# Selection matrices compared with a row of numbers in PSUM, in a two-layer graph network kernel

## The chip, the cores and the metric

The kernel runs on one core of a Trainium2 chip. The metric is the device time of one execution in microseconds (us), start to end on that core; lower is better. The core has a matrix engine (TensorE, PE in the profile, its weight loads PEld), a vector engine (VectorE, DVE), a scalar engine (ScalarE, ACT), a general engine (GpSimd, POOL) which here mainly issues gathers from memory, and a queue that issues other transfers (SyncE, SP). SBUF is the on-chip memory, PSUM the smaller memory that TensorE writes its results to, in eight banks.

## What is computed

There are 12500 nodes with 64 features each and 212500 edges, sorted by destination. A first layer adds, for each node, the features of the sources of its edges and the edges' own features, and runs a small network and a batch norm on the sum. A second and a third layer are graph convolutions on the same edges. Cut to what matters:

```python
edge_index = jnp.stack([src, dst])
h = jnp.maximum(_layernorm(x), 0.0)
# layer 0
msg = h[src] + edge_attr_64
agg = jax.ops.segment_sum(msg, dst, num_segments=n)
y = jax.nn.relu(agg @ W1 + b1) @ W2 + b2
x = x + batch_norm(y)
h = jnp.maximum(_layernorm(x), 0.0)
# layer 1, twice: h -> relu(segment_sum((h @ W)[src] * enorm, dst) + b)
...
x = x + layer_norm_over_the_graph(h)
```

The edges' sum by destination is the work: it is done three times, once in each of three passes.

## The kernel before

Each of the three passes (numbered 0, 1 and 2) adds, for every node, the rows of its sources in two ways.

**Dense tiles.** For the first 54 tiles of 125 destination nodes in pass 0 (69 in passes 1 and 2) a matrix of counts, sources by destinations, is built and multiplied with the node rows held in SBUF. A tile has 25 slots. In a slot of a built tile DVE makes a pair of one-hot matrices (`oh`: L906 from `modT`, L907 from `keyT`), PE multiplies them (`bld`, L1030), and ACT copies the result to SBUF as a slice of the counts (`evict`, L1150). PE applies a finished tile's counts to the node rows, four matmuls in each slot (`app`, L1048). When a tile is done, DVE folds its three parts (`fold_v`, L947 and L948), PE turns the fold over (`turn`, L1135) into `ps_g`, the first 128 columns of PSUM bank 6, and DVE adds that to the sums in `acc` (`add`, L968).

**Groups.** The edges of the other nodes, and in pass 0 the edge features of all edges, go in groups of 1280 edges (128 partitions by 10). DVE makes a selection matrix `S` for a group (L917): 128 x 10 x 96 numbers, 1 where an edge's destination relative to the group's first is equal to the column's number. In pass 0 it also splits the edges' features in three parts (`rest1` and `rest2`, both L931). PE multiplies `S` with the edge features (L1063, pass 0) and with the gathered rows (L1070), ten matmuls each. POOL issues the gathers, ten to a group, into four buffers (L1212). DVE folds the result (`fold_q`, L938), PE turns it into `ps_g` (L1131), and DVE adds it to a window of `acc` (`add`, L964). Pass 0 has 167 groups, of which 79 gather; passes 1 and 2 have 54 each, and all gather.

**What sets the order.** `make_plan` gives each step of a pass a number in slots, and each engine's list is sorted by it. Each engine then works strictly down its list, with semaphore waits. For a group that PE takes at `t`, `S` stands at `t - 5.6`, `rest1` at `t - 5.2`, `rest2` at `t - 4.2`, `fold_q` at `t + 2.4`, its turn at `t + 4.6`, its add 2.1 behind the turn. A pair of one-hots stands 3.3 ahead of its build. A tile's fold stands 2.7 ahead of its turn or more. In pass 0 there are 1387 slots, and groups follow each other every 8.23 slots.

**Buffers that tie the engines.** There are four pairs of one-hots (`NOH`): DVE makes a pair once the build four before is done. There are three banks for builds (`NBANK`), two buffers of `S` (`NS`), two folds of each kind, and one `ps_g`, so a turn waits for the add before it.

## Time and profile before

| | |
|---|---|
| median of 3 runs | 4285.88 us |
| lowest, highest run | 4264.55, 4296.05 us |
| the profiled execution | 4260.3 us |
| its span, first to last instruction | 4258.7 us |
| PE, DVE, ACT, POOL busy in the span | 73%, 43%, 32%, 51% |
| granted TensorE clock, mean | 0.83 of full speed |

The profile is of one execution. Pass 0 lies between 160 and 1740 us of its span, pass 1 between 1880 and 3125, pass 2 between 3125 and 4215. A busy share over the whole span mixes these passes, in which different engines are loaded, so the windows by stage are to be read first. "Idle before" is the time in which an engine had nothing to run ahead of an instruction, and the name behind the arrow is what ended it; "issue" is time for which no releaser is seen, "remote" stands for one that the profile does not know.

### The profile page before, as it was taken

The numbers are of one execution on the slowest core, as the hardware profiler recorded it, in microseconds if no ns is written. First come the engines' busy times: TensorE is split into PE (matmuls) and PEld (weight loads), VectorE is DVE, ScalarE is ACT, GpSimd is POOL, SyncE is SP. The second block draws the span as 40 slices with busy tenths as digits, with TensorE's granted clock in tenths as the row PEclk, the third lists the DMA queues.
The fourth block names the chain that finished last, engine by engine and source line by source line (L and its number), as shares of the span: only waits on it lengthen the run. The fifth ranks groups of instructions, "written<-read, shape, count | busy, mean of one in ns | idle before, by whom it ended". The sixth has DMA issues, their size and how long they took to land.

```text
span 4258.7 us, 67106 instructions
## 1 busy us (share of the span) xinstructions
PE 3105.3 (73%) x25880; PEld 2681.6 (63%) x25880; DVE 1824.2 (43%) x5570; ACT 1353.1 (32%) x2188; POOL 2185.3 (51%) x1905
## 2 busy tenths in 40 slices
PE   2466877878777788557777787877847777777776
PEld 1245666666566676446776676766847766677666
DVE  7656777778676778612323232332201111111112
ACT  1345665656555666432223232222200000000001
POOL 5676777787767670034444444444144444444541
PEclk6678999989888899678878888888968878888888
DMA  3433444444444343543233333333543333333434
GB/s 65 103 104 103 127 123 127 121 113 130 115 106 123 108 131 110 110 136 127 92 134 102 122 127 101 132 103 118 163 123 116 123 126 118 122 128 117 135 116 128
DMA packets 396698, 503.75 MB, mean 118 GB/s; under 512 B 340668, under 2 KB 340732, under 8 KB 371676
## 3 DMA queue, kind: packets, MB, share of 16 engines
q1 hardware_dynamic: 323345, 402.81, 29.5%
q0 software_dynamic: 60416, 93.34, 9.0%
q10 hardware_dynamic: 12616, 3.20, 0.5%
q8 instruction: 216, 3.54, 0.3%
q14 instruction: 105, 0.86, 0.1%
HBM read 362.07 MB, written 137.13 MB: 117 GB/s over the span
## 4 chain that ended last, share of the span: by engine, by line
PE 53%; DVE 15%; another core or an unknown queue 12%; issue 12%; POOL 3%; ACT 2%; DVEq 1%; DMA 0%; SPq 0%; ACTq 0%; POOLq 0%
PE psum L1048 33%; PE psum L1030 8%; PE psum L1070 4%; DVE arena L907 4%; PE psum L1063 4%; DVE arena L917 3%; DVE arena L931 3%; DVE arena L906 2%; PE psum L1015 1%; POOL arena L1212 1%; ACT arena L1150 1%; DVEq L962 1%; PE psum L1135 1%; PE psum L1083 1%
## 5 line engine op out<-in xcount | busy, mean ns | idle before, releaser
L1212 POOL DMA_INDIRECT arena<-table,srcT x1840 | 2090.4, 1136 | 1709.7 <-PE psum L1070 1056.0
L1048 PE MATMUL psum<-arena 125*125 125x193 bf16 (+1 forms) x19200 | 2323.0, 266 | 369.0 <-issue 316.4
L1048 PEld LDWEIGHTS psum<-arena 125*125 125x125 fp8e4 x19200 | 2090.6, 151 | 609.7 <-issue 458.5
L1150 ACT ACTIVATE arena<-psum 125x500 fp8e4<-125x500 f32 x1775 | 1156.9, 709 | 1355.8 <-PE psum L1030 948.6
L1030 PE MATMUL psum<-arena 128*125 128x500 f16 x1775 | 735.9, 416 | 271.5 <-issue 108.1
L906 DVE TENSOR_SCALAR arena<-iota,modT 128x125 f16<-128x125 f16 x1775 | 468.3, 264 | 544.2 <-PE psum L1030 287.4
L907 DVE TENSOR_SCALAR arena<-iota,keyT 128x500 f16<-128x500 f16 x1775 | 617.3, 348 | 0.0
L1030 PEld LDWEIGHTS psum<-arena 128*125 128x125 f16 x1775 | 259.0, 146 | 377.7 <-DVE arena L907 193.4
L1194 ACT ACTIVATE cneg<-cst 125x1 f32<-125x1 f32 x25 | 5.1, 203 | 1135.4 <-DVE arena L987 950.8
L917 DVE TENSOR_TENSOR arena<-relT,iota 128x960 bf16<-128x960 f16 x272 | 311.2, 1144 | 0.0
L948 DVE TENSOR_REDUCE arena<-psum 125x64 f32<-125x192 f32 x192 | 67.1, 350 | 515.6 <-remote 302.8
L931 DVE TENSOR_TENSOR arena<-arena 128x650 f32<-128x650 f32 (+1 forms) x334 | 274.0, 820 | 0.9 <-DMA arena<-in_edge_attr_dram 0.8
L938 DVE TENSOR_REDUCE arena<-psum 96x65 f32<-96x195 f32 (+1 forms) x275 | 96.2, 350 | 272.0 <-PE psum L1070 268.6
L1070 PE MATMUL psum<-arena 128*96 128x192 bf16 x1846 | 198.8, 259 | 10.1 <-DMA arena<-table,srcT 9.9
L1063 PE MATMUL psum<-arena 128*96 128x195 bf16 (+1 forms) x1662 | 204.1, 275 | 2.1 <-DVE arena L931 1.7
L1135 PE MATMUL psum<-ident,arena 125*64 125x125 f32 x192 | 60.5, 315 | 197.0 <-DVE arena L948 97.1
L1063 PEld LDWEIGHTS psum<-arena 128*96 128x96 bf16 (+1 forms) x1662 | 181.2, 137 | 8.0 <-issue 5.8
L1070 PEld LDWEIGHTS psum<-arena 128*96 128x96 bf16 x1846 | 176.6, 132 | 11.8 <-DMA arena<-table,srcT 10.7
L968 DVE SCALAR_TENSOR_TENSOR acc<-psum,acc 64x125 f32<-64x125 f32 x192 | 53.3, 277 | 264.7 <-remote 171.9
L947 DVE COPY cnt<-psum 125x1 f32<-125x1 f32 x123 | 18.8, 153 | 341.5 <-remote 243.1
L1135 PEld LDWEIGHTS psum<-ident,arena 125*64 125x64 f32 x192 | 23.6, 123 | 219.1 <-issue 179.7
L964 DVE TENSOR_TENSOR acc<-acc,psum 65x96 f32 (+1 forms) x275 | 67.6, 246 | 191.6 <-PE psum L1131 141.4
(199 smaller groups left out, 1008.3 us busy)
## 6 DMA issues: line engine op xcount, KB each, us to landing
arena<-counts SPq DMA_DIRECT2D x121, 1600.0 KB
counts<-arena SPq DMA_DIRECT2D x71, 1600.0 KB
arena<-in_edge_attr_dram SPq DMA_DIRECT2D x166, 320.0 KB
arena<-table,srcT POOLq DMA_INDIRECT x1840
table<-arena SPq DMA_DIRECT2D x8, 1050.0 KB
table<-arena SPq DMA_DIRECT2D x25, 168.0 KB
arena<-table SPq DMA_DIRECT2D x4, 1050.0 KB
arena<-in_x_dram ACTq DMA_DIRECT2D x4, 700.0 KB
```

Source lines behind the costliest of these rows:

```text
L906: dve.tensor_scalar(ob(v % NOH), iota0[:, 0:PN], modT[:, v:v + 1], None, ALU.is_equal)
L907: dve.tensor_scalar(oh(v % NOH), iota1[:, :], keyT[:, v:v + 1], None, ALU.is_equal).then_inc(v_oh, 1)
L917: dve.tensor_tensor(S, rel, it, ALU.is_equal).then_inc(v_S, 1)
L931: dve.tensor_tensor(ebuf(e, i + 1)[0:parts, 0:nt * FE], a, upper, ALU.subtract).then_inc(v_rest1 if i == 0 else v_rest2, 1)
L938: dve.tensor_reduce(qbuf(n % 2)[:, 0:fe], ps_q.rearrange("p (s f) -> p f s", s=3)[:, 0:fe, :], X, ALU.add).then_inc(v_fq, 1)
L1030: pe.matmul(ps_b[v % NBANK][0:PN, :], ob(v % NOH), oh(v % NOH), start=True, stop=True).then_inc(p_bld, 1)
L1048: last = pe.matmul(ps_v[n % 2][0:PN, 0:xc], A(slot)[0:PN, j, 0:PN], Xs[0:PN, j, 0:xc], start=(j == 0), stop=(j == J - 1))
L1063: last = pe.matmul(ps_q, S[0:parts, t, :], e3(v % NEDGE)[0:parts, t, :, :], start=(t == 0), stop=(t == nt - 1 and not gathered))
L1070: last = pe.matmul(to, S[0:parts, t, :], gbuf(slot)[0:parts, t, :].rearrange("p (s f) -> p s f", s=3), start=(k > 0 and t == 0), stop=(t = ...
L1135: pe.transpose(ps_g[0:F, 0:PN], vbuf(m % 2)[0:PN, :], ident[0:PN, 0:PN]).then_inc(p_win, 1)
L1150: act.activation(A(slot)[0:PN, :, i * SUB:(i + 1) * SUB], ps_b[b % NBANK][0:PN, :].rearrange("p (j r) -> p j r", r=SUB), ACT.Copy, scale=S ...
L1212: pool.indirect_dma_start(out=gbuf(slot)[0:parts, t, :], out_offset=None, in_=tables[k], in_offset=bass.IndirectOffsetOnAxis(ap=idx, axis= ...
```

## The change

Four edits. First, a row of numbers 0 to 95 in 32-bit floats (`ps_i`) is written once into columns 256 to 351 of PSUM bank 6, beside `ps_g`. Second, `S` is made by a `scalar_tensor_tensor` that adds 0 to the relative destinations (16-bit, SBUF) and compares the result with `ps_i`, in place of a `tensor_tensor` on two 16-bit operands in SBUF. Third, since DVE now reads bank 6 for `S` and PE writes the turns there, `S` waits until PE has done the turn of the last fold that stands ahead of it in DVE's list, and `S` stands at `t - 7.0` in place of `t - 5.6`. Fourth, the add of a group takes the form that the add of a tile has: `scalar_tensor_tensor` with the PSUM operand first.

```diff
@@ make_plan
-        dve.append((t - 5.6, "S", n))
+        dve.append((t - 7.0, "S", n))
@@
         ps_g = psum[:, 6, 0:P]
+        ps_i = psum[:, 6, 2 * P:2 * P + W]
@@ dve_enter
+                V(dve.tensor_copy(ps_i, iota[:, 0:W]))
@@ dve_pass
-            for kind, v in half(pl, "dve", early):
+            whole = pl["dve"]
+            folded = [0]
+            for kind, v in whole:
+                u = pl["turn"]["grp" if kind == "fold_q" else "win", v] + 1 if kind in ("fold_q", "fold_v") else 0
+                folded.append(max(folded[-1], u))
+            first = 0 if early is not False else pl["early"]["dve"]
+            for at, (kind, v) in enumerate(half(pl, "dve", early), first):
@@ kind == "S"
                     if n >= NS:
                         dve.wait_ge(p_q, n - NS + 1)
+                    if folded[at]:
+                        dve.wait_ge(p_win, pl["u0"] + folded[at])
                     S = sbuf(n % NS)
                     if g < G:
                         rel = relT[:, :, g:g + 1].broadcast_to([P, NT, W])
-                        it = iota0[:, 0:W].rearrange("p (a w) -> p a w", a=1).broadcast_to([P, NT, W])
-                        dve.tensor_tensor(S, rel, it, ALU.is_equal).then_inc(v_S, 1)
+                        it = ps_i.rearrange("p (a w) -> p a w", a=1).broadcast_to([P, NT, W])
+                        dve.scalar_tensor_tensor(out=S, in0=rel, scalar=0.0, in1=it, op0=ALU.add,
+                                                 op1=ALU.is_equal).then_inc(v_S, 1)
...
@@ kind == "add"
-                        dve.tensor_tensor(win, win, ps_g[0:fe, 0:W], ALU.add).then_inc(v_add, 1)
+                        dve.scalar_tensor_tensor(out=win, in0=ps_g[0:fe, 0:W], scalar=1.0, in1=win, op0=ALU.mult,
+                                                 op1=ALU.add).then_inc(v_add, 1)
```

DVE's list in pass 0 around the `S` of group 75 (the groups counted from 0 in the order in which they are taken). Before:

```order
L906 TENSOR_SCALAR arena<-iota,modT 128x125
L907 TENSOR_SCALAR arena<-iota,keyT 128x500
L906 TENSOR_SCALAR arena<-iota,modT 128x125
L907 TENSOR_SCALAR arena<-iota,keyT 128x500
L938 TENSOR_REDUCE arena<-psum 96x65
L906 TENSOR_SCALAR arena<-iota,modT 128x125
L907 TENSOR_SCALAR arena<-iota,keyT 128x500
L917 TENSOR_TENSOR arena<-relT,iota 128x960
L931 TENSOR_TENSOR arena<-arena 128x650
L906 TENSOR_SCALAR arena<-iota,modT 128x125
L907 TENSOR_SCALAR arena<-iota,keyT 128x500
L931 TENSOR_TENSOR arena<-arena 128x650
```

And of the change, whose line numbers are higher by 8 to 13 (L914 and L915 are the pair, L927 is `S`, L950 `fold_q`, L943 the rests):

```order
L914 TENSOR_SCALAR arena<-iota,modT 128x125
L915 TENSOR_SCALAR arena<-iota,keyT 128x500
L927 SCALAR_TENSOR_TENSOR arena<-relT,psum 128x960
L914 TENSOR_SCALAR arena<-iota,modT 128x125
L915 TENSOR_SCALAR arena<-iota,keyT 128x500
L950 TENSOR_REDUCE arena<-psum 96x65
L914 TENSOR_SCALAR arena<-iota,modT 128x125
L915 TENSOR_SCALAR arena<-iota,keyT 128x500
L943 TENSOR_TENSOR arena<-arena 128x650
L914 TENSOR_SCALAR arena<-iota,modT 128x125
L915 TENSOR_SCALAR arena<-iota,keyT 128x500
L943 TENSOR_TENSOR arena<-arena 128x650
```

`S` has moved ahead of a pair of one-hots, of `fold_q` and of a second pair. Over pass 0 it moves ahead of two pairs for 65 of the 167 groups, of one pair for 99, and of none for 3.

DVE's list in pass 0 around the `S` of group 28, where a tile's fold stands near. Before (L947 and L948 are the tile's count and fold):

```order
L947 COPY cnt<-psum 125x1
L948 TENSOR_REDUCE arena<-psum 125x64
L906 TENSOR_SCALAR arena<-iota,modT 128x125
L907 TENSOR_SCALAR arena<-iota,keyT 128x500
L938 TENSOR_REDUCE arena<-psum 96x65
L906 TENSOR_SCALAR arena<-iota,modT 128x125
L907 TENSOR_SCALAR arena<-iota,keyT 128x500
L917 TENSOR_TENSOR arena<-relT,iota 128x960
```

And of the change (L959 and L960 are the tile's count and fold):

```order
L959 COPY cnt<-psum 125x1
L960 TENSOR_REDUCE arena<-psum 125x64
L927 SCALAR_TENSOR_TENSOR arena<-relT,psum 128x960
L914 TENSOR_SCALAR arena<-iota,modT 128x125
L915 TENSOR_SCALAR arena<-iota,keyT 128x500
L950 TENSOR_REDUCE arena<-psum 96x65
L914 TENSOR_SCALAR arena<-iota,modT 128x125
L915 TENSOR_SCALAR arena<-iota,keyT 128x500
```

`S` now stands right behind the tile's fold, so it waits there until PE has done that fold's turn. In 30 of the 167 groups of pass 0, and in 9 of the 54 of each later pass, `S` stands between a fold and the add behind its turn; in the others the wait is for a turn whose add DVE has already done.

## Rows read from the trace of the kernel before

**Rows 1.** Windows by stage: stretch, its length, busy us of each engine (instructions), granted clock.

```profile
160.00:1740.00 1580.00, 1229.76 (x9515) 985.37 (x9515) 1147.44 (x3703) 913.65 (x1493) 1065.97 (x783) 0.89 0.43 118
1880.00:3125.00 1245.00, 969.14 (x8389) 866.41 (x8389) 357.59 (x1301) 330.79 (x509) 491.50 (x507) 0.84 0.37 122
3125.00:4215.00 1090.00, 808.09 (x7410) 754.54 (x7411) 139.04 (x336) 17.68 (x66) 500.57 (x518) 0.82 0.37 122
```

**Rows 2.** Waits of PE in the first pass: us in total, times, longest us.

```profile
PE psum L1030 <- issue: 88.3, 68, 6.9
PE psum L1030 <- ACT arena L1150: 80.7, 57, 14.5
PE psum L1030 <- DVE arena L907: 62.4, 130, 4.5
...
PE psum L1070 <- DMA arena<-table,srcT: 9.9, 3, 5.8
```

**Rows 3.** Waits of DVE in the first pass, same columns.

```profile
DVE arena L906 <- PE psum L1030: 239.9, 202, 4.6
```

**Rows 4.** Waits of PE in the second and third pass, same columns.

```profile
PE psum L1048 <- issue: 295.3, 453, 2.5
...
PE psum L1030 <- DVE arena L907: 14.5, 9, 3.2
```

**Rows 5.** Page, costliest groups: count, busy us, mean ns, idle before and its releaser.

```profile
L1212 POOL DMA_INDIRECT arena<-table,srcT x1840 | 2090.4, 1136 | 1709.7 <-PE psum L1070 1056.0
...
L917 DVE TENSOR_TENSOR arena<-relT,iota 128x960 bf16<-128x960 f16 x272 | 311.2, 1144 | 0.0
...
L931 DVE TENSOR_TENSOR arena<-arena 128x650 f32<-128x650 f32 (+1 forms) x334 | 274.0, 820 | 0.9 <-DMA arena<-in_edge_attr_dram 0.8
...
L968 DVE SCALAR_TENSOR_TENSOR acc<-psum,acc 64x125 f32<-64x125 f32 x192 | 53.3, 277 | 264.7 <-remote 171.9
...
L964 DVE TENSOR_TENSOR acc<-acc,psum 65x96 f32 (+1 forms) x275 | 67.6, 246 | 191.6 <-PE psum L1131 141.4
```

**Rows 6.** Two DVE forms at 256 columns, line L983: ns min/median/max.

```profile
L983 DVE SCALAR_TENSOR_TENSOR arena<-psum,dis x25: 405/425/426, 1929.2 to 3072.8; 125x256 f32<-125x256 f32 x25
```

**Rows 7.** The other form at 256 columns, line L996: ns min/median/max.

```profile
L996 DVE TENSOR_TENSOR arena<-arena x25: 409/425/473, 1934.3 to 3075.0; 125x256 bf16<-125x256 f32 x25
```

**Rows 8.** Timeline of DVE around group 75: start us, us, instruction, idle before.

```profile
892.33 0.26 DVE L906 TENSOR_SCALAR arena<-iota,modT 128x125 f16<-128x125 f16 x1 [0.97 <-PE psum L1030]
...
893.45 1.15 DVE L917 TENSOR_TENSOR arena<-relT,iota 128x960 bf16<-128x960 f16 x1
894.51 0.83 DVE L931 TENSOR_TENSOR arena<-arena 128x650 f32<-128x650 f32 x1
...
895.68 0.83 DVE L931 TENSOR_TENSOR arena<-arena 128x650 f32<-128x650 f32 x1
```

**Rows 9.** Timeline of PE in the same stretch.

```profile
892.47 0.38 PE L1030 MATMUL psum<-arena 128*125 128x500 f16 x1
...
893.03 0.37 PE L1030 MATMUL psum<-arena 128*125 128x500 f16 x1
...
895.82 0.42 PE L1030 MATMUL psum<-arena 128*125 128x500 f16 x1 [0.32 <-DVE arena L907]
...
896.99 0.43 PE L1030 MATMUL psum<-arena 128*125 128x500 f16 x1 [0.40 <-DVE arena L907]
```

**Rows 10.** Timeline of POOL there.

```profile
891.41 0.95 POOL L1212 DMA_INDIRECT arena<-table,srcT  x1 [0.30 <-issue]
...
893.96 4.95 POOL L1212 DMA_INDIRECT arena<-table,srcT  x1 [0.30 <-issue]
```

**Rows 11.** Windows of POOL line L1212 alone, by pass.

```profile
160.00:1740.00 1580.00, 1065.88 (x782) 0.89 0.43 118
1880.00:3125.00 1245.00, 491.50 (x507) 0.84 0.37 122
```

**Rows 12.** Timeline of DVE, a fold of a tile ahead of group 28.

```profile
462.86 0.35 DVE L948 TENSOR_REDUCE arena<-psum 125x64 f32<-125x192 f32 x1
...
466.37 1.15 DVE L917 TENSOR_TENSOR arena<-relT,iota 128x960 bf16<-128x960 f16 x1
```

**Rows 13.** Timeline of PE there: the turn of that fold, and a build.

```profile
467.79 0.27 PE L1135 MATMUL psum<-ident,arena 125*64 125x125 f32 x1
...
468.45 0.37 PE L1030 MATMUL psum<-arena 128*125 128x500 f16 x1
```

5 lines of the change are left out of this document (3 added, 2 removed).

## The prediction

> **What bounds the kernel now.** I read the windows by stage first. Pass 0 is the only stage in which DVE (1147 us of 1580), PE (1230) and POOL (1066) are all heavily loaded; in pass 2 DVE works 139 us of 1090 [rows 1]. So each pass needs its own reading.
>
> In passes 1 and 2 PE sets the time. Its long wait is "issue", 295.3 us, for which no engine is named; for a pair of one-hots it waits 14.5 us in both together [rows 4]. What DVE does faster, or POOL, finds no one waiting there.
>
> In pass 0 no single engine is full. PE waits 62.4 us for the one-hots (130 times), 80.7 us for ACT's copies, 88.3 us for "issue", and 9.9 us for gathers [rows 2]. DVE in its turn waits 239.9 us, 202 times, for a build on PE to free a pair of buffers [rows 3]. The two stop each other in turn. The timeline shows one cycle. DVE stands 0.97 us ahead of 892.33 while PE works through a group; then come a pair, the fold, a pair, `S` at 893.45, the first rest at 894.51, a pair, the second rest at 895.68 [rows 8]. PE, whose builds follow each other at 0.56 us (892.47, 893.03), runs out of pairs and stands 0.32 us at 895.82 and 0.40 us at 896.99 [rows 9]. DVE has too little to do during a group's matmuls and too much just behind them. That is the stretch in which the change moves `S`.
>
> **The form of `S`.** One of 960 columns takes 1144 ns, with nothing idle ahead of it [rows 5]. The slope between L931, 650 columns in 820 ns, and L917 is 324 ns for 310 columns, 1.045 ns each; so `S` is 1003 ns of columns and 141 fixed. The trace has no `scalar_tensor_tensor` of 960 columns with one operand in PSUM. The nearest are L968, 125 columns in 277 ns, which is 131 and 146 fixed [rows 5], and L983, 256 columns, median 425 ns [rows 6], against 425 ns for a `tensor_tensor` of 256 columns with both in SBUF [rows 7]. At the same size the price is the same. I see no gain from below, since every one of these forms costs 1.04 ns a column or more; from above, the slope from L968 to L983, (425 - 277) / 131 = 1.13 ns, would make `S` 1220 ns, 76 ns more, for 167 of them in pass 0 13 us of DVE. I take 0, since L983 is nearest in size and equal, and keep +13 for the range.
>
> The Trainium skill, page "VectorE: DVE Perf Modes", section "The TRN2 errata", gives a fixed 58 cycles for SBUF sources and 120 for PSUM sources, which as an estimate is 65 ns more for each `S`, 11 us in pass 0. The fixed terms of L931 and L968, 141 and 146 ns, do not show that difference.
>
> **The add of a group.** 246 ns at 96 columns is 100 and 146 fixed; L968 has 146 too [rows 5]. No change. The row of numbers costs one small instruction before pass 0, below 0.3 us.
>
> **What POOL gets.** A gather takes 1065.88 / 782 = 1.36 us in pass 0 and 491.50 / 507 = 0.97 in pass 1 [rows 11]. At group 75 one begins at 893.96, beside `S` and both rests, and takes 4.95 us, where one beside an idle or lightly loaded DVE took 0.95 [rows 10]. So something in DVE's work holds the gathers up, 0.39 x 782 = 305 us in all. `S` takes 1.06 us from its start to the next one's [rows 8], and DVE works 1147 us for 167 groups, 6.9 us each [rows 1]: `S` is about a sixth, so I give the new form some 50 us of POOL's time in pass 0. Who waits for it? PE waits 9.9 us for gathers in the whole pass, 3 times [rows 2], and the page has POOL itself waiting 1056 us for free buffers over the three passes [rows 5]. The waits are those of the first groups, before POOL is ahead. I take 4 us, with 0 and 9.9 as ends. Were the cover gone, that is, POOL no longer ahead, the gain would be the larger number, but nothing shows it.
>
> The Trainium skill, page "SBUF — State Buffer", section "Who interferes with whom", says that a `tensor_tensor` with two SBUF inputs contends with what GpSimd reads, and infers that it does not hold up the making of descriptors. By that the new form gives POOL nothing, and my 4 us would be 0. The gather of 4.95 us ran beside `tensor_tensor` for 2.8 us, but beside one-hot pairs as well, so the trace leans against the inference without settling it.
>
> **`S` moved to t - 7.0.** It now goes ahead of two pairs in 65 of 167 groups. At group 75 it would run in the idle time before 892.33: 0.97 us of its 1.06 us would cost nothing, and the pairs behind the rests would come 0.97 us earlier, which is more than the 0.32 and the 0.40 us that PE stood. Where it passes one pair only, DVE has mostly begun to run again when it comes to `S`, and the sum of work up to the late pairs is the same as before. So the share of PE's 62.4 us that goes is about 65 / 167 = 0.39, or 24 us; I take 21, since in some of these groups ACT's copy is what PE would find late next. The ends are 0 (ACT or "issue" takes all of it) and 62 us. Nothing waits for `S` longer: it is made earlier than before for the same use at `t`.
>
> **The new wait.** In 30 groups of pass 0 `S` stands between a fold and the add behind its turn. Queued behind it on DVE are a pair, `fold_q`, a second pair and the rests; PE waits for the pairs. Where PE has already done the turn, the cost is 0. The worst that I can place is group 28: the tile's fold ends at 463.21, its turn on PE at 468.06 [rows 12, 13], so `S` is held 4.85 us. It then ends its share at 469.12 and the next pair takes 0.43 more, to 469.55, while PE, which had four pairs in hand, would want that one at 468.45 [rows 13]. PE stands 1.1 us. So 30 holds cost between 0 and 33 us. I take 9, 0.3 us each, since with most of them the turn is at most a slot or two off and PE keeps a pair in hand. The 18 holds of passes 1 and 2 stand where PE hardly asks for pairs [rows 4]: 0, at most 5 us.
>
> **Sum.** -21 (place) -4 (gathers) +9 (holds) = -16 us on the profiled 4260.3 us, 4244. The profiled execution is 0.6% below the median of the three runs, 4285.88, so the forecast for a median is 4285.88 - 16 = 4270 us. A difference within 1%, 43 us, is about what a measurement of this kernel can't tell from none.
>
> **The rivals.**
>
> *Holds decide (slower).* The mechanism is the wait for `p_win` on DVE at `S`. For it: at group 28 DVE is held 4.85 us, and a late pair lets PE, then ACT, then DVE slip together, so that one hold may cost more than its own 1.1 us. Against it: in the cycle shown DVE is late, not early, and PE passes the turn before DVE asks. At 1.1 us for each of 48 holds, with the +13 us of a dearer `S` and none of the gains, it gives +66, 4352 us; it turns the sum positive from 0.8 us for each of the 30. With half of that, 4319.
>
> *The place gives nothing (same).* PE's waits for the pairs change into waits for ACT, already the larger number, or "issue" [rows 2]. Then +5 to -5: 4285 us.
>
> *More of the pass comes loose (faster by over 1%).* All 62.4 us for the pairs go, and with them some of the waits for ACT, which gets its builds later whenever PE is late. No holds cost: -62 -10 = -72, 4214 us; with half of ACT's 80.7 as well, 4173.
>
> *POOL is the thing.* The 50 us of gathers come off the pass, beside the 16. Against it stand the 9.9 us of PE's waits. It would give 4220 us.
>
> **How the numbers follow.** The forecast's own case, a small gain of 5 to 40 us, I give 0.40; nothing gained or lost within 1%, 0.22; the larger gain 0.20 and POOL's 0.04; holds that cost over 1% 0.14. The range leaves out the outer half of the gains and the end of the holds: 4215 to 4325 us. Faster by over 1%: 0.25; within 1%: 0.61; slower by over 1%: 0.14.
>
> **What the profile of the changed kernel would show.** The `S` instruction has a mean between 1140 and 1150 ns; 1220 would show the dearer form. The group's add stays near 246 ns. Gathers in pass 0 fall from 1.36 us to about 1.30; PE's wait for gathers stays below 10 us. PE's wait for the second one-hot falls from 62.4 to about 40 us in pass 0, and DVE's wait ahead of the first falls from 239.9 by some 60 (65 groups by 0.97), since `S` fills it; idle time ahead of `S`, 0 before, appears with PE's tile turn as its releaser, some 30 us in pass 0. Passes 1 and 2 keep 1245 and 1090 us within 10. The forecast is wrong if pass 0 changes by more than 40 us, or if the time ahead of `S` is above 60 us.

## The result, and the profile of the changed kernel

The change takes 4315.75 us, median of 9 runs (4296.81 to 4324.11), against 4279.65 us for the kernel before in 9 runs (4245.02 to 4296.05). The ratio is 1.0088, with a 95% interval of 1.0057 to 1.0119: slower by 0.9%, 36 us, where the forecast was a gain of 16 us. The time lies inside the forecast range, on the other side of no change. The profiled execution took 4301.35 us (span 4299.8, granted clock 0.827); that of before 4260.3 (4258.7, 0.833).

The page of the changed kernel first, its costliest groups: count, busy us and mean ns, idle before and what ended most of it.

```profile
L1225 POOL DMA_INDIRECT arena<-table,srcT x1840 | 1913.6, 1040 | 1917.9 <-PE psum L1083 1281.2
L1061 PE MATMUL psum<-arena 125*125 125x193 bf16 (+1 forms) x19200 | 2338.2, 268 | 406.5 <-issue 357.5
...
L927 DVE SCALAR_TENSOR_TENSOR arena<-relT,psum 128x960 bf16<-128x960 f16 x272 | 311.2, 1144 | 68.8 <-PE psum L1148 61.4
...
L943 DVE TENSOR_TENSOR arena<-arena 128x650 f32<-128x650 f32 (+1 forms) x334 | 274.0, 820 | 5.2 <-DMA arena<-in_edge_attr_dram 2.9
...
L981 DVE SCALAR_TENSOR_TENSOR acc<-psum,acc 64x125 f32<-64x125 f32 x192 | 53.2, 277 | 254.2 <-remote 171.0
...
L976 DVE SCALAR_TENSOR_TENSOR acc<-psum,acc 65x96 f32 (+1 forms) x275 | 68.7, 250 | 198.1 <-PE psum L1144 153.8
```

`S` takes 1144 ns, as before, and the add of a group 250 ns against 246 [rows 5]. A gather fell from 1136 to 1040 ns. What grew is the idle time ahead of PE's `app` (L1061): its largest part, "issue" (no releaser seen), is 357.5 us. In the page of before the same line has 316.4, on 369.0 idle in all.

PE's waits in pass 0 of the changed kernel: us in total, times, longest us.

```profile
PE psum L1043 <- issue: 105.1, 62, 27.5
PE psum L1043 <- ACT arena L1163: 69.6, 57, 3.8
PE psum L1043 <- DVE arena L915: 42.0, 59, 4.6
...
PE psum L1083 <- DMA arena<-table,srcT: 5.8, 1, 5.8
```

And DVE's waits there.

```profile
DVE arena L914 <- PE psum L1043: 238.0, 199, 8.9
...
DVE arena L927 <- PE psum L1148: 33.0, 18, 5.4
```

Against rows 2, PE waits 42.0 us for pairs instead of 62.4, and 69.6 for ACT instead of 80.7: the step that was forecast. But "issue" ahead of builds grew by 16.8 us, to 105.1. DVE's wait for a build stayed at 238.0 us (239.9 in rows 3), and 33.0 us of idle time appeared ahead of `S`, the longest 5.4 us. Two places in DVE's timeline, first the fold ahead of group 28 and its `S` (start us, us, instruction, idle before):

```profile
469.82 0.35 DVE L960 TENSOR_REDUCE arena<-psum 125x64 f32<-125x192 f32 x1
475.55 1.15 DVE L927 SCALAR_TENSOR_TENSOR arena<-relT,psum 128x960 bf16<-128x960 f16 x1 [5.38 <-PE psum L1148]
```

and then group 75 and the pairs on either side of its `S`:

```profile
916.75 0.26 DVE L914 TENSOR_SCALAR arena<-iota,modT 128x125 f16<-128x125 f16 x1 [0.38 <-PE psum L1043]
...
917.18 1.15 DVE L927 SCALAR_TENSOR_TENSOR arena<-relT,psum 128x960 bf16<-128x960 f16 x1
919.05 0.26 DVE L914 TENSOR_SCALAR arena<-iota,modT 128x125 f16<-128x125 f16 x1 [0.72 <-PE psum L1043]
```

At group 28 `S` is held 5.38 us. At group 75 the idle time has not gone: 0.38 us stand ahead of the pair before `S` and 0.72 ahead of the pair behind it.

PE's waits in passes 1 and 2:

```profile
PE psum L1061 <- issue: 342.9, 495, 2.5
PE psum L1148 <- DVE arena L960: 104.7, 26, 17.8
```

"issue" ahead of `app` is 342.9 us against 295.3 [rows 4]. Ahead of PE's other lines it fell by 22 us in the same windows, so that 26 of the 48 are left in all, and they lie in pass 2. To compare the passes at equal work I use the fold of a tile as a mark: pass 2 is measured from its first to its last fold of a tile, here from the starts of L948 (before) and L960 (change) in the trace. The line as a whole, first of before, then of the change (the last start is the end of pass 2's stretch):

```profile
L948 DVE TENSOR_REDUCE arena<-psum x192: 334/348/359, 224.1 to 4227.7; 125x64 f32<-125x192 f32 x192
```

```profile
L960 DVE TENSOR_REDUCE arena<-psum x192: 335/348/359, 272.6 to 4268.8; 125x64 f32<-125x192 f32 x192
```

The first folds of pass 2 start at 3107.3 us and at 3124.5 us. So pass 2 lasts 4227.7 - 3107.3 = 1120.4 us before and 4268.8 - 3124.5 = 1144.3 us changed: 24 us, in a pass that the prediction held to be untouched. With marks of the same kind pass 1 goes from 1187.8 to 1200.0, and pass 0 (from the first build to the last fold) from 1571.2 to 1577.9.

The waits of PE in these two stretches of pass 2, before and then changed:

```profile
PE psum L1048 <- issue: 183.2, 257, 2.5
PE psum L1135 <- DVE arena L948: 52.0, 14, 7.2
```

```profile
PE psum L1061 <- issue: 219.2, 294, 2.5
PE psum L1148 <- DVE arena L960: 46.8, 14, 7.4
```

"issue" ahead of `app` grew by 36 us; ahead of PE's other lines it fell by 7, so the growth is 29 us in all, from 216 to 245. No other wait of PE there grew by more than 2. The gathers, by pass (before, the third pass has 500.57 us for 518, in rows 1):

```profile
160.00:1740.00 1580.00, 904.53 (x782) 0.88 0.44 117
1880.00:3145.00 1265.00, 494.35 (x514) 0.83 0.38 120
3145.00:4240.00 1095.00, 487.23 (x516) 0.81 0.37 120
```

In pass 0 a gather takes 904.53 / 782 = 1.16 us against 1.36 [rows 11], in pass 2 487.23 / 516 = 0.944 against 500.57 / 518 = 0.966. The change as a whole frees the gathers, in pass 0 by 0.20 us each where the prediction put down 0.06.

**Where the "issue" waits lie.** The timeline of pass 2 of the kernel before, PE:

```profile
3326.65 5.09 PE L1048 MATMUL psum<-arena 125*125 125x192 bf16 x53
3332.53 0.54 PE L1048 MATMUL psum<-arena 125*125 125x192 bf16 x4 [0.80 <-issue]
3333.96 0.58 PE L1048 MATMUL psum<-arena 125*125 125x192 bf16 x5 [0.88 <-issue]
3335.39 0.49 PE L1048 MATMUL psum<-arena 125*125 125x192 bf16 x4 [0.85 <-issue]
3336.11 0.24 PE L1048 MATMUL psum<-arena 125*125 125x192 bf16 x1 [0.23 <-issue]
3336.83 0.74 PE L1048 MATMUL psum<-arena 125*125 125x192 bf16 x3 [0.48 <-issue]
3338.24 2.08 PE L1048 MATMUL psum<-arena 125*125 125x192 bf16 x12 [0.68 <-issue]
```

and POOL, in the same stretch:

```profile
3324.03 0.95 POOL L1212 DMA_INDIRECT arena<-table,srcT  x1 [6.77 <-PE psum L1070]
3325.29 0.94 POOL L1212 DMA_INDIRECT arena<-table,srcT  x1 [0.30 <-issue]
3326.53 0.95 POOL L1212 DMA_INDIRECT arena<-table,srcT  x1 [0.30 <-issue]
3327.79 0.95 POOL L1212 DMA_INDIRECT arena<-table,srcT  x1 [0.31 <-issue]
3329.04 1.37 POOL L1212 DMA_INDIRECT arena<-table,srcT  x1 [0.30 <-issue]
3330.71 0.95 POOL L1212 DMA_INDIRECT arena<-table,srcT  x1 [0.31 <-issue]
```

POOL issues ten gathers in a run, from 3324.03 to 3336.66. PE works for the first half of it, then stops six times, for 3.92 us in all, until just behind its end. The fifth gather takes 1.37 us where its neighbours take 0.95: `S` began at 3328.44. In pass 2 every one of PE's waits for "issue" begins between the first gather of a run and 3 us behind its last one, in both kernels. Counted from the two traces, per unbroken run of gathers:

| pass 2 | runs with an `S` beside them | PE's "issue" in one | runs without | in one |
|---|---|---|---|---|
| before | 20 | 3.48 us | 31 | 4.73 us |
| changed | 24 | 4.92 us | 27 | 4.71 us |

The column "runs without" is not of one kind. It holds a run of forty gathers, the first four groups of the pass, from 3106.95 us on before. PE waits 36.9 us beside it before and 37.0 changed. After the first stops it gets one matmul in where 2.8 us pass:

```profile
3147.73 0.32 PE L1048 MATMUL psum<-arena 125*125 125x192 bf16 x1 [2.48 <-issue]
3150.53 0.32 PE L1048 MATMUL psum<-arena 125*125 125x192 bf16 x1 [2.48 <-issue]
3153.33 0.32 PE L1048 MATMUL psum<-arena 125*125 125x192 bf16 x1 [2.48 <-issue]
```

The 29 and 25 runs of ten without an `S` have 3.78 and 3.55 us. So the form is read from the same runs of ten in both kernels. The 20 that have an `S` beside them in both have 3.48 us of "issue" before and 4.93 changed; the 25 that have one in neither have 3.57 and 3.55. An old `S` beside a run takes some 1.4 us off the wait that PE has beside the new one. The gathers show the other side: a run of ten takes 12.20 us without an `S` and 12.20 beside a new one, but 12.77 beside an old one. That is the theory that the runs tested: what the old `S` holds up is worth time to PE.

### The profile page after: what moved, and what is told of

Read it like the earlier page. It is cut to its first block, busy times and chain, and to the rows that moved or that the text cites. A ratio compares the mean times of both kernels' runs of the same rounds, so it can differ in the third digit from the quotient of the medians.

```text
span 4299.8 us, 67380 instructions
## 1 busy us (share of the span) xinstructions
PE 3124.5 (73%) x25880; PEld 2701.7 (63%) x25880; DVE 1822.3 (42%) x5571; ACT 1353.0 (31%) x2188; POOL 2009.4 (47%) x1905
## 4 chain that ended last, share of the span: by engine, by line
PE 54%; issue 14%; DVE 13%; another core or an unknown queue 12%; ACT 2%; POOL 2%; DVEq 1%; DMA 1%; SPq 0%; ACTq 0%; POOLq 0%
PE psum L1061 34%; PE psum L1043 8%; PE psum L1083 4%; PE psum L1076 3%; DVE arena L915 3%; DVE arena L943 3%; DVE arena L914 2%; ACT arena L1163 2%; PE psum L1028 1%; DVEq L974 1%; PE psum L1148 1%; PE psum L1096 1%; POOL acc L624 1%; DVE arena L927 1%
## 5 line engine op out<-in xcount | busy, mean ns | idle before, releaser
L1225 POOL DMA_INDIRECT arena<-table,srcT x1840 | 1913.6, 1040 | 1917.9 <-PE psum L1083 1281.2
L1061 PE MATMUL psum<-arena 125*125 125x193 bf16 (+1 forms) x19200 | 2338.2, 268 | 406.5 <-issue 357.5
L1061 PEld LDWEIGHTS psum<-arena 125*125 125x125 fp8e4 x19200 | 2108.8, 152 | 639.9 <-issue 490.8
L914 DVE TENSOR_SCALAR arena<-iota,modT 128x125 f16<-128x125 f16 x1775 | 463.7, 261 | 507.1 <-PE psum L1043 285.5
L915 DVE TENSOR_SCALAR arena<-iota,keyT 128x500 f16<-128x500 f16 x1775 | 617.0, 348 | 0.0
L927 DVE SCALAR_TENSOR_TENSOR arena<-relT,psum 128x960 bf16<-128x960 f16 x272 | 311.2, 1144 | 68.8 <-PE psum L1148 61.4
L960 DVE TENSOR_REDUCE arena<-psum 125x64 f32<-125x192 f32 x192 | 67.2, 350 | 540.0 <-PE psum L1061 294.6
L943 DVE TENSOR_TENSOR arena<-arena 128x650 f32<-128x650 f32 (+1 forms) x334 | 274.0, 820 | 5.2 <-DMA arena<-in_edge_attr_dram 2.9
L950 DVE TENSOR_REDUCE arena<-psum 96x65 f32<-96x195 f32 (+1 forms) x275 | 96.2, 350 | 265.8 <-PE psum L1083 264.2
L959 DVE COPY cnt<-psum 125x1 f32<-125x1 f32 x123 | 18.9, 153 | 336.9 <-remote 211.3
L976 DVE SCALAR_TENSOR_TENSOR acc<-psum,acc 65x96 f32 (+1 forms) x275 | 68.7, 250 | 198.1 <-PE psum L1144 153.8
```

What stands on the lines that cost most here:

```text
L914: dve.tensor_scalar(ob(v % NOH), iota0[:, 0:PN], modT[:, v:v + 1], None, ALU.is_equal)
L915: dve.tensor_scalar(oh(v % NOH), iota1[:, :], keyT[:, v:v + 1], None, ALU.is_equal).then_inc(v_oh, 1)
L927: dve.scalar_tensor_tensor(out=S, in0=rel, scalar=0.0, in1=it, op0=ALU.add, op1=ALU.is_equal).then_inc(v_S, 1)
L943: dve.tensor_tensor(ebuf(e, i + 1)[0:parts, 0:nt * FE], a, upper, ALU.subtract).then_inc(v_rest1 if i == 0 else v_rest2, 1)
L950: dve.tensor_reduce(qbuf(n % 2)[:, 0:fe], ps_q.rearrange("p (s f) -> p f s", s=3)[:, 0:fe, :], X, ALU.add).then_inc(v_fq, 1)
L1061: last = pe.matmul(ps_v[n % 2][0:PN, 0:xc], A(slot)[0:PN, j, 0:PN], Xs[0:PN, j, 0:xc], start=(j == 0), stop=(j == J - 1))
```

## The experiments

The chips on which the runs fell are of two sorts: on three of them the kernel before takes 4278 to 4388 us, as in the result above (I call them A), on two 3261 and 3263 us (B). Each run is compared only with runs of before on its own chip, and what is told of the two sorts stands apart. A kernel's time is the median of its runs, and each ratio has its 95% interval behind it. "Pass 0, 1, 2" are the stretches between folds defined above, from the profiled execution; pass 1 is the same code in the kernel before and in e2_pass0, and lasted 1187.8 and 1212.1 us; pass 2, the same in both too, lasted 1120.4 and 1120.3. So the medians decide, pass 2 shows where, and pass 1 shows little.

### The parts, on a chip of sort A (before: 4277.89 us, 35 runs)

**e1_place**, the kernel before with only the place of `S` changed:

```diff
-        dve.append((t - 5.6, "S", n))
+        dve.append((t - 7.0, "S", n))
```

> The kernel before with S placed at t - 7.0 in place of t - 5.6, nothing else; no wait is added and S keeps its old form. If the place is what costs, this shows most of the +36 us (ratio 1.006 to 1.010). If the place does what my forecast said, it gains: -10 to -30 us. If the wait or the form costs, this is within 5 us of before.

Measured: 4256.41 us, 0.9949 (0.9917 to 0.9982): -21 us, the forecast's term. Pass 2 is 1123.2 us. For pass 0 the trace to compare with is that of e3_pass12 (below), which has the old code there and ran on the same chip. DVE's wait for builds, in e3_pass12 and then in e1_place:

```profile
DVE arena L914 <- PE psum L1057: 254.6, 204, 8.8
```

```profile
DVE arena L906 <- PE psum L1030: 208.5, 171, 5.8
```

PE's wait for pairs falls from 70.7 to 51.1 us. A gather in pass 0 falls from 1346 to 1286 ns, by the place alone.

**e2_pass0**, the change in pass 0 alone, with the old place, form and add in the others, and **e3_pass12**, with `k > 0` for `k == 0`, the change in passes 1 and 2 alone:

```diff
-        dve.append((t - 7.0, "S", n))
+        dve.append((t - (7.0 if k == 0 else 5.6), "S", n))
...
+                    if k == 0:
...
+                    else:
...
+                            dve.tensor_tensor(S, rel, it, ALU.is_equal).then_inc(v_S, 1)
...
+                        if k == 0:
...
+                        else:
+                            dve.tensor_tensor(win, win, ps_g[0:fe, 0:W], ALU.add).then_inc(v_add, 1)
```

> The change (place, form, wait and add) in pass 0 alone; passes 1 and 2 as before. The profile of the change had +7 us in pass 0, +12 in pass 1, +22 in pass 2. If the loss arises in each pass by what is done in it, this gives +7 us (ratio 1.001 to 1.003). If the loss in the later passes is carried over from pass 0 or comes from how the program lies in memory, it gives +20 to +40.

> The change in passes 1 and 2 alone; pass 0 as before. If the loss is made in each pass by itself: +25 to +35 us (ratio 1.006 to 1.008), with PE's issue waits in pass 2 up by some 30 us. If those waits differ only by chance from execution to execution: within 8 us of before.

Measured: 4274.97 us, 1.0009 (0.9972 to 1.0046), and 4302.61, 1.0062 (1.0027 to 1.0098). In pass 0 the change gives 3 us, which is nothing within the noise, where the place alone, put in all passes, gives 21; in passes 1 and 2 it costs 25 us. Pass 2 is 1120.3 us in e2_pass0, with the old form there, and 1141.0 in e3_pass12, with the new.

**e4_nohold**, the change, with `S` moved ahead of the fold whose turn it would wait for:

```diff
+    while at < len(dve):
+        if dve[at][0] == "S":
+            to, open_turn = at, None
+            for j in range(at - 1, -1, -1):
+                if dve[j][0] in ("fold_q", "fold_v"):
+                    u = turn["grp" if dve[j][0] == "fold_q" else "win", dve[j][1]]
+                    if ("add", u) in dve[:at]:
+                        break
+                    to = j
+            dve.insert(to, dve.pop(at))
+        at += 1
```

> The changed kernel with every S that stood between a fold and the add behind its turn moved ahead of that fold, so that the new wait never holds DVE. If the holds cost (30 in pass 0, 9 in each later pass): 4275 to 4290 us. If the form of S and the adds cost, or POOL's freer gathers do: 4305 to 4320, as the change. The 69 us of idle time ahead of S should fall to near 0 in either case.

Measured: 4316.94 us, 1.0104 (1.0073 to 1.0135), as the change itself (1.0088). The idle time ahead of `S` is 0.0 us in its trace, for 68.8 with the holds, and the time is no lower. So the holds cost nothing that shows, to within some 15 us either way. That was my rival on the slower side, and it does not carry the loss.

### The form and the add, on chips of sort B (before: 3263.04 us, 23 runs; 3260.76, 17 runs)

The next eight runs ask whether the add, the instruction or its operand does it, and what the gathers cost PE. On this sort of chip PE has no "issue" waits in any pass, so they answer for a case that the theory has not met. What they say of the time holds for this sort alone.

**e5_add** (the new add alone) and **e6_form_sbuf** (the new instruction for `S`, both operands in SBUF, old place):

```diff
-                        dve.tensor_tensor(S, rel, it, ALU.is_equal).then_inc(v_S, 1)
+                        dve.scalar_tensor_tensor(out=S, in0=rel, scalar=0.0, in1=it, op0=ALU.add, op1=ALU.is_equal).then_inc(v_S, 1)
...
```

> The kernel before with the add of a group in the tile's form, and nothing else. Theory now: what costs in passes 1 and 2 is that the new form of S no longer holds up POOL's gathers, and that PE's issue waits, which lie beside the gathers, get longer for it. The add's form did not change how long gathers beside it take (0.73 of its time before, 0.60 after, in a fit of gather times over what DVE ran beside them), so by this theory: no change, within 10 us of before. Rival: the add's form is the cause, then +20 us, most of it in pass 2.

> The kernel before with S made by scalar_tensor_tensor, both operands still in SBUF, at t - 5.6, no wait. If it is the second operand in SBUF that holds up the gathers, they stay at 1.36 us in pass 0 and the time stays within 10 us of before. If it is the form of the instruction: gathers fall to 1.16 us in pass 0, and the time rises by 20 to 45 us.

Measured: 3263.43 us, 1.0004 (0.9984 to 1.0024), and 3259.08, 0.9987 (0.9969 to 1.0005). Neither moves the time. In both, a gather in pass 0 takes 1431 ns. So neither the instruction nor the add frees the gathers. With `ps_i` as the second operand (f1_change, below) one takes 1230, but f1_change has the new place too, and part of this fall is the place's: on sort A the place alone took 60 ns off a gather in pass 0 (e1_place) and the rest of the change another 126 (e4_nohold, 1160). Pass 2 is free of this, since the place changes nothing there: a gather takes 991 ns in e5_add, 993 in e6_form_sbuf and 943 in f1_change. It is the operand read from PSUM, and not the instruction, that frees them.

**e8_nogather2** and, on the second of these chips, **f2_nogather2**: before, without the gathers of pass 2.

```diff
-                        pe.wait_ge(d_gat[slot], gat_sum[k, v])
+                        if k < 2:
+                            pe.wait_ge(d_gat[slot], gat_sum[k, v])
...
-                pool_gather(k, i)
+                if k < 2:
+                    pool_gather(k, i)
```

PE's wait for them goes too, and it multiplies what lies in the buffers, so the third pass adds wrong rows: the kernel leaves out work that the result needs.

> The kernel before without the gathers of pass 2: PE multiplies what lies in the buffers from before, so the third pass adds wrong rows. Theory: PE's issue waits of pass 2 (216 us) are made by the gathers, so they fall below 40 us and pass 2 from 1120 us to 930 or less. Rival: PE's instructions come too slowly by themselves, then the waits stay above 150 us and pass 2 above 1080.

> The kernel before without the gathers of pass 2: PE multiplies what lies in the buffers from before, so the third pass adds wrong rows. Theory: PE's issue waits of pass 2 (216 us, where before is near 4280) are made by the gathers, so they fall below 40 us and pass 2 from 1120 us to 930 or less. Rival: PE's instructions come too slowly by themselves, then the waits stay above 150 us and pass 2 above 1080. Where before is near 3263 there are no such waits to remove, and the whole gives 3190 to 3210.

Measured, one run each: 3197.48 and 3199.03 us, 66 and 62 us less; pass 2 goes from 713 (e5_add) to 650.5 us.

**e9_both12** and **f3_both12**: the change, with `S` made in the old form first and then again in the new one, in passes 1 and 2.

```diff
+                        if k > 0:
+                            it = iota0[:, 0:W].rearrange("p (a w) -> p a w", a=1).broadcast_to([P, NT, W])
+                            V(dve.tensor_tensor(S, rel, it, ALU.is_equal))
                         it = ps_i.rearrange("p (a w) -> p a w", a=1).broadcast_to([P, NT, W])
```

> The change, with S in passes 1 and 2 made twice at its new place: first in the old form on two operands in SBUF, then again in the new form. It adds work to DVE, 108 times 1.1 us. Theory (what a two-operand instruction in SBUF takes from POOL, it gives to PE): passes 1 and 2 come back, pass 2 from 1144 us to about 1122, in all 4285 to 4295 us. Rival (the read of PSUM, the wait or the place costs): no gain, 4310 to 4330.

> The change, with S in passes 1 and 2 made twice: first in the old form on two operands in SBUF, then again in the new form. Theory, where before is near 4280: pass 2 comes back from 1144 us to about 1122, in all 4285 to 4300 us. Rival (the read of PSUM, the wait or the place costs there): no gain over the change, 4310 to 4330. Where before is near 3263: as the change or 0 to 25 us above it, since gathers are then held up for nothing.

Measured: 3166.85 us, 0.9701 (0.9674 to 0.9729), and 3162.68, 0.9692 (0.9661 to 0.9723). They are read beside f1_change, next.

**f1_change**, the change itself, and **f4_twice12**, before with `S` made twice in the old form in passes 1 and 2:

```diff
+                        if k > 0:
+                            for _ in range(1):
+                                V(dve.tensor_tensor(S, rel, it, ALU.is_equal))
                         dve.tensor_tensor(S, rel, it, ALU.is_equal).then_inc(v_S, 1)
```

> The change itself, once more. The four runs before this one (the add, the form in SBUF, no gathers, both forms) went to a chip on which the kernel before takes 3263 us and PE has no issue waits at all; those before them to one on which it takes 4278 us and PE has 500 us of them. Theory: what the new form of S takes away is a hold on POOL's gathers. Where PE has issue waits beside gathers (before near 4280), PE pays for it: 4305 to 4320, ratio 1.006 to 1.011. Where it has none (before near 3263) POOL bounds pass 0, and the change gains: 3150 to 3190, ratio 0.965 to 0.98.

> The kernel before, with S in passes 1 and 2 made twice in its old form at its old place, 108 more instructions of 1.1 us on DVE. Theory: a second hold on the gathers is worth as much as the first was: 10 to 30 us less than before where before is near 4280, most of it in pass 2. Rival (the new form costs by something of its own, not by what it lets go): no gain, 0 to 5 us more. Where before is near 3263: 0 to 20 us more.

Measured: f1_change 3119.78 us, 0.9559 (0.9529 to 0.9588); f4_twice12 3273.68, 1.0025 (1.0005 to 1.0045). On this sort the same change is 4.4% faster: pass 0 goes from about 1445 us (e5_add, which is as before) to 1327.7, pass 2 from 713 to 687.8. No run here has the place alone, so the 117 us of pass 0 are the whole change's. An old `S` costs here and gives nothing back: f3_both12 loses 43 us against f1_change, and f4_twice12 is 13 us above before. f4_twice12 was meant for sort A, where the theory wanted 10 to 30 us less of it with no read of PSUM in play; it was not run there, so that test is open. The chain of e5_add, the page's shares of the span by engine and by line:

```profile
POOL 50%; PE 28%; issue 14%; DVE 5%; DMA 2%; SPq 1%; ACT 1%; DVEq 0%; POOLq 0%; ACTq 0%
POOL arena L1213 48%; PE psum L1049 19%; PE psum L1031 3%; PE psum L1071 2%; POOL acc L623 1%; DMA arena<-table,srcT 1%; PE psum L1016 1%; POOL acc L604 1%; PE psum L1064 1%; DVE arena L917 1%; DVE arena L907 0%; DVE arena L931 0%; SPq L122
```

and the waits of PE in its pass 0:

```profile
PE psum L1071 <- DMA arena<-table,srcT: 81.0, 30, 6.3
PE psum L1031 <- DVE arena L907: 79.1, 180, 4.5
```

The chain and PE's waits of f1_change, which answer to them:

```profile
PE 43%; POOL 21%; DVE 18%; issue 12%; DMA 3%; ACT 1%; DVEq 1%; SPq 1%; POOLq 0%; ACTq 0%
PE psum L1061 24%; POOL arena L1225 19%; PE psum L1043 6%; DVE arena L915 5%; DVE arena L943 4%; PE psum L1076 4%; PE psum L1083 3%; DVE arena L914 3%; DMA arena<-in_edge_attr_dram 2%; DVE arena L927 1%; DVEq L974 1%; POOL acc L624 1%; DVE 
```

```profile
PE psum L1043 <- DVE arena L915: 46.6, 86, 5.3
...
PE psum L1083 <- DMA arena<-table,srcT: 12.8, 5, 5.6
```

Half of the chain is POOL, and PE waits 81.0 us in 30 places for gathers, 12.8 with the change. PE catches POOL up here, so a freed gather is time won. On sort A, PE waits 9.9 us for gathers [rows 2], so there is hardly a wait for a freed gather to shorten.

### The gathers and PE, on a second chip of sort A (before: 4381.76 us, 29 runs)

**g1_nogather2** (the kernel of e8_nogather2), **g2_both12** (that of e9_both12), **g3_place** (that of e1_place) and **g4_nohold** (that of e4_nohold) repeat their kernels on a chip with "issue" waits. The passes 0 and 1 of g1_nogather2 are those of before.

> The kernel before without the gathers of pass 2 (the third pass adds wrong rows), wanted on the kind of chip on which before takes near 4280 us. Theory: the gathers make PE's issue waits of pass 2 (216 us), so they fall below 40 us and pass 2 from 1120 us to 930 or less. Rival: they stay above 150 us and pass 2 above 1080. Where before is near 3260: 3190 to 3210 again.

> The change with S in passes 1 and 2 made in the old form and then again in the new one. Theory, where before is near 4280: pass 2 comes back from 1144 us to about 1122, in all 4285 to 4300. Rival (the read of PSUM, the wait or the place): 4310 to 4330. Where before is near 3260: 3155 to 3170 again.

> The kernel before with S at t - 7.0 and nothing else. Where before is near 4280 it was 0.9949 of before and is so again. Where before is near 3260, pass 0 is bound by gathers as by PE and DVE, and the place frees none: 0 to 25 us less (ratio 0.992 to 1.000). Rival: the place is the larger part of the change's -141 us there, then 60 us or more less.

> The change with every S that would be held by the new wait moved ahead of the fold. Where before is near 4280 it was level with the change (4317) and is so again. Where before is near 3260: the holds cost what they cost, 0 to 15 us, so 3105 to 3120 against the change's 3120.

Measured: g1_nogather2 3889.94 us in one run, 492 us less. The whole of pass 2 without gathers, and with them in g3_place (stretch, its length, busy us of PE, PEld, DVE, ACT and POOL with instructions, granted clock, DMA share, GB/s):

```profile
3207.00:3858.00 651.00, 648.32 (x7648) 645.58 (x7645) 142.28 (x347) 19.29 (x72) 0.00 (x0) 1.00 0.49 173
```

```profile
3175.00:4323.00 1148.00, 838.78 (x7642) 780.00 (x7639) 141.41 (x346) 19.30 (x72) 515.60 (x531) 0.81 0.38 121
```

Without gathers PE is busy 648.32 us of 651, at a granted clock of 1.00. With them the same matmuls keep it busy 838.78 us, at 0.81, so some 190 of the 498 us between the two are matmuls that take longer, beside the 236 us of "issue". Pass 2 lasts 650.5 us, to the tenth what it lasts without gathers on sort B. With them it lasts 1148.3 us here (g3_place) and 713 on sort B. So the difference between the two sorts in this pass comes with the gathers: they cost 498 us on one, 63 on the other.

g3_place: 4356.59 us, 0.9934 (0.9898 to 0.9969), -25 us: the place again. In pass 0, g1_nogather2 to g3_place, PE's wait for pairs falls from 73.1 to 43.2 us, DVE's for builds from 252.1 to 194.5, and a gather from 1347 to 1259 ns. g4_nohold: 4404.57, 1.0058 (1.0025 to 1.009). Pass 2 is 1148.3 us in g3_place, with "issue" 236 us, and 1176.2 in g4_nohold, with 261.

g2_both12: 4410.78 us, 1.0061 (1.0032 to 1.009). With the old `S` made as well, "issue" in pass 2 falls from 261 to 229 us and the pass from 1176.2 to 1164.7, but pass 1 is no shorter (1253.9 against 1247.9) and the total is that of g4_nohold. In the 20 runs of ten with an `S` beside them in both, "issue" is 5.15 us in g4_nohold and 4.12 with the old `S` made as well. So it takes part of PE's waits away, as the theory has it, but not the time: 12 of 28 us in pass 2 and none in the total, which is what the rival (the read of PSUM, the wait or the place) said. Its extra 1.14 us of DVE for each of 108 groups, and a hold that it has and g4_nohold lacks, stand against it; I can't divide them. This test is half a confirmation.

### More runs of gathers beside an `S` (sort A, before: 4387.55 us, 17 runs)

**h1_place_split** is e1_place, and **h2_change_split** the change, with the ten gathers of a group in passes 1 and 2 issued in two halves, the second half waiting for the second turn behind that of the group which frees the buffer:

```diff
             for t in range(nt):
+                if pause and t == NT // 2:
+                    pool.wait_ge(p_win, pause)
```

> The kernel before with S at t - 7.0, and in passes 1 and 2 each group's ten gathers in two halves: the second five wait until PE has done two more turns. In the traces where before takes 4280 us or more, PE's issue waits begin 5 to 6 us after POOL begins a group of ten, which is after some four gathers, and end 2 us after the last. Theory (a long unbroken run of gathers is what starves PE): issue waits of pass 2 fall from 216 to 236 us to below 120, pass 2 by 50 to 150 us. Rival (each gather costs PE the same wherever it stands): pass 2 within 15 us of 1148 or 1123. Where before is near 3260 PE has no such waits; there it costs 0 to 60 us, since POOL loses its lead.

> The change with the same split of the gathers in passes 1 and 2. Theory as for the other: where before is near 4280 or above, 50 to 200 us below the change in passes 1 and 2 together. Rival: level with the change (1.006 to 1.011 of before). Where before is near 3260: 3120 to 3180.

Measured: h1_place_split 4301.61 us, 0.9826 (0.9794 to 0.9859), -86 us; h2_change_split 4371.14, 0.9983 (0.996 to 1.0006). The split did not do what I meant it to: "issue" in pass 2 is 223 and 263 us, where below 120 was expected. A run is still ten gathers long, in pass 2 12.2 to 13.3 us: the second half of a group now goes together with the first half of the next. What changed is where the runs stand. Per run of gathers, as in the table above:

| | pass | with an `S` beside | in one | without | in one | pass lasts |
|---|---|---|---|---|---|---|
| g3_place (old form) | 2 | 20 | 3.91 us | 31 | 5.09 us | 1148.3 us |
| g4_nohold (new) | 2 | 28 | 5.17 us | 23 | 5.06 us | 1176.2 us |
| h1_place_split (old) | 1 | 21 | 3.02 us | 29 | 3.46 us | 1196.1 us |
| h2_change_split (new) | 1 | 19 | 4.33 us | 31 | 3.36 us | 1218.9 us |
| h1_place_split (old) | 2 | 30 | 3.78 us | 21 | 5.21 us | 1119.1 us |
| h2_change_split (new) | 2 | 31 | 5.10 us | 20 | 5.22 us | 1155.4 us |

In pass 2 the column "without" again holds the run of forty, with 37.7 to 38.8 us; its runs of ten have 3.6 to 4.1. Run by run, where both kernels of a pair have an `S` beside a run of ten: 3.28 and 4.81 us in 24 runs of e1_place and e4_nohold, 3.91 and 5.15 in 20 of g3_place and g4_nohold, 3.82 and 5.16 in 29 of the two with the split. And where the second of a pair alone has one, a new one, it changes nothing: 5.01 and 4.98 us in 8 runs (e1, e4), 5.18 and 5.23 in 8 (g3, g4). So it is the old `S` that takes something off, and not the new one that adds. With 30 runs covered instead of 20, the form is worth 36 us in pass 2 instead of 28. Why the split gains more than that (0.9826 with the old form, where the place alone gave 0.9949 and 0.9934) isn't settled; it is seen in pass 1 too, where the runs beside an `S` are 21 instead of 4. This is the version that beats the kernel before on sort A by the most; on sort B it wasn't tried, and there the change as it is (0.9559) is the best that ran.

## Why the prediction was wrong, by its own steps

**The place of `S`: right.** The term was -21 us; e1_place gives -21, g3_place -25. That it agrees so closely is luck, since the interval of e1_place goes from -36 to -8 us. The mechanism is the one forecast: with the place alone no idle time stands around the `S` of group 75 in either trace, DVE's wait for builds falls by 46 and 58 us against the old code on the same chip (some 60 forecast), and PE's wait for pairs by 20 and 30 (22 forecast). In the changed kernel part of this is gone again. DVE's wait for builds is 238.0 us, and 0.38 and 0.72 us of idle time stand on either side of `S` at group 75. With the holds taken out as well it is 246.2 and 232.7 (e4_nohold, g4_nohold), so it is not the holds that bring it back. What in the rest of the change does was not tried by itself.

**The form, its price on DVE: right.** 1144 ns for 1144. By the Trainium skill, page "VectorE: DVE Perf Modes", section "The TRN2 errata", with its fixed 58 cycles for SBUF and 120 for PSUM sources, it would have been 1209 as an estimate; the trace does not show it. The add: 250 ns for 246, and no time on sort B (e5_add). On sort A it was not run alone.

**The new wait: within its bounds.** +9 us was put down, between 0 and 33. e4_nohold takes it away and gains nothing, so no cost shows; with the intervals as wide as they are, 9 us would not show either. Idle time ahead of `S` was 33.0 us in pass 0 with PE's turn as its releaser, forecast as 30. The worst hold was 5.38 us, forecast as 4.85.

**What POOL gets: the step that failed.** I wrote: "What DVE does faster, or POOL, finds no one waiting there", and -4 us for the gathers with 0 and 9.9 as ends. First, the relief was larger: 0.20 us a gather in pass 0 (0.06 forecast), 160 us in all. The form's part of it is 0.126 us (e1_place to e4_nohold) or 0.107 (g3 to g4), 84 to 99 us in all for the 50 that I gave it; the rest is the place's, for which I had put down nothing. I had shared 305 us out by DVE's busy time, but a us of `S` does not hold up as much as a us of anything else: a run of ten beside an old `S` of 1.14 us takes 0.57 us longer in pass 2, beside a new one no longer at all. My reading of group 75 had a slip as well. The gather of 4.95 us begins 0.51 us behind `S` and so ran beside `S` and the rests for 2.3 us, not 2.8, which changes no term. The Trainium skill, page "SBUF — State Buffer", section "Who interferes with whom", infers that a `tensor_tensor` with two SBUF inputs does not hold up the making of descriptors. These traces contradict it, if the gather's time on POOL is that making: 12.77 us a run beside the old `S` and 12.20 beside the new one or none. Second, and this turned the sign, the ends of the term stopped at zero. I asked who waits for POOL and not whom POOL disturbs. PE's 295.3 us of "issue" in passes 1 and 2 [rows 4] stood in my own rows as time "for which no engine is named", and I left it there. In pass 2 it lies entirely beside the gathers, and where the gathers are relieved it grows: 216 us to 245 in the pass, 24 us of time. The prediction's own sign for this, that passes 1 and 2 keep their time within 10 us, failed with 12 and 24. Its two named signs of being wrong, 40 us in pass 0 and 60 us ahead of `S`, did not show it.

**The sum, as it came out.** Place -21. Form in pass 0: e2_pass0 less the whole of e1_place, -3 against -21, so about +18, a difference about as large as its own uncertainty. Passes 1 and 2: +25 (e3_pass12). Together +22; measured +36. The intervals are some 15 us to either side each. With the place held nearly equal on one chip (e4 and g4 move some `S` further ahead), form and add together cost 60.5 us (e4_nohold less e1_place), 48.0 (g4 less g3) and 69.5 (h2 less h1).

**The rivals.** "Holds decide" had the right sign and the wrong mechanism. "POOL is the thing" I gave 0.04: false on sort A. On sort B pass 0 gave 117 us while PE's wait for gathers there fell from 81.0 to 12.8 and POOL's share of the chain from 50% to 21%. I had drawn the evidence against it, 9.9 us of PE's waits, from a chip of sort A, and for that sort it was sound.

**What is shown and what is not.** Shown: PE's "issue" waits in pass 2 lie beside runs of gathers and go with them (g1_nogather2). With the new form of `S` they are longer, by 1.2 to 1.5 us in each run of ten that has an `S` beside it in both kernels, and on average unchanged in the runs that have one in neither (3.57 and 3.55 us before and changed). Pass 2 is longer by 21 to 36 us (before and changed, e2 and e3, e1 and e4, g3 and g4, h1 and h2). In pass 1 only 4 to 11 runs have an `S` beside them without the split, too few to tell. Argued only: that PE gains because a held-up gather leaves PE's instructions room. g2_both12 agrees with it in PE's waits and by half in pass 2, and not in the total, and the cleanest test, f4_twice12 on sort A, was not run. How a gather keeps PE from issuing stays open. Transfers of instructions (queue 8, 216 in either kernel) take 1.0 to 1.1 us each before, changed and on sort B, so their own duration does not explain it; how long one waited before it began is not in the trace. Why two sorts of chips differ was not tried.

## What to carry to other kernels

Ask of a relieved engine not only who waits for it but who is disturbed by what it does sooner: put the waits without a named cause beside the timeline of every other engine before calling them a constant. Where "issue" waits of a matrix engine line up with the gathers, an instruction that slows the gathers can be worth its time. Before two classes of stretches are compared by their means, look for one member that makes the mean, as the run of forty did here, and match them one by one. And try a change on more than one chip: this one is worth -4.4% on one sort and +0.9% on the other.

## What the runs showed of the hardware

- Gathers issued by POOL can cost PE far more than the waits for their data: pass 2 lasts 650.5 us without them and 1148.3 with them on one sort of chip, 713 on the other. On the first, PE stops beside a run of ten (12.2 to 13.3 us) for 3.3 to 5.2 us on average, in stops of 0.7 to 0.8 us. The first stop mostly comes 5 to 9 us behind the first gather, and the last ends some 2 us behind the last gather's end, or earlier. Beside a run of forty (49.8 us) it stops for 37.
- The granted clock is lower where PE stops: 1.00 in pass 2 without gathers, 0.81 with them. At the run of forty in the kernel before, the first stop is at 3113.7 us, the clock goes from 2.4 to 1.2 GHz at 3118.0 and back at 3169.2, when PE's waits have ended (3163.8). So the 498 us between g1_nogather2 and g3_place are more than the 236 of "issue": the same matmuls keep PE busy 839 us for 648.
- A DVE instruction of 960 columns (1.14 us) with two operands in SBUF lengthens a run of ten gathers from 12.20 to 12.77 us (12.88 on a second chip), 0.5 to 0.6 us for each us of it; with the second operand in PSUM it leaves 12.20 (before and changed, g3_place and g4_nohold, pass 2).
